# Orders at the end of the first attention and on the way to the second mixer's keys, places of two key jobs, and counts without zero matmuls

## The chip, the cores and the metric

The kernel runs on one core of a Trainium2 chip. The metric is the device time of one execution in microseconds (us). The core has engines that run side by side, each through its own list of instructions in order: TensorE (PE in the views, with its weight loads as PEld), VectorE (DVE), ScalarE (ACT), GpSimd (POOL) and SyncE (SP, which only issues DMAs here). They wait for one another on semaphores alone. TensorE writes to PSUM, from where VectorE and ScalarE take the results to SBUF.

## The reference

1024 tokens with 512 features each go through two layers of a graph network. 16384 edges (`src`, `dst`) are given, sorted by `dst`. Cut to what matters here:

```python
edge_index = jnp.stack([src, dst])
xn = _layernorm(x)
x = x + gnn0(xn, edge_index) + mixer0(xn)     # gnn0: dense attention under an adjacency mask
x = x + ffn0(_layernorm(x))                   # weight replaced by its sign, output rounded to sevenths
xn = _layernorm(x)
x = x + gnn1(xn, edge_index) + mixer1(xn)     # gnn1: 2 layers of 8-head edge attention; mixer1: linear attention
x = x + ffn1(_layernorm(x))                   # small per-row networks on nibbles

# gnn0
adj = jnp.zeros((N, N)).at[edge_index[0], edge_index[1]].set(1.0)
a = q @ k.T / sqrt(D)
a = a * adj + (1.0 - adj) * NEG
out = softmax(a) @ v
# mixer1, the second mixer
q, k, v = split(x @ Wqkv)                     # to 8 heads
q = elu(q) + 1.0;  k = elu(k) + 1.0
kv = einsum('bhnd,bhne->bhde', k, v)
z = 1.0 / (einsum('bhnd,bhd->bhn', q, k.sum(axis=2)) + 1e-06)
out = (einsum('bhnd,bhde->bhne', q, kv) * z) @ Wout + bout
# gnn1, for each of 2 layers: scores of each edge, softmax over the edges of one target, weighted sum of the values
scores = jnp.einsum('ehd,ehd->eh', q[tgt], k[srcidx])
```

How often each pair (source, target) occurs is a 1024 x 1024 table, which the kernel builds once and uses as the mask of the first attention and, in its logarithm, as the weight of each pair in the second network's attention.

## The kernel before

One function, `build`, holds a list of instructions for each engine, in the order in which its author wrote them. Nothing reorders them. What TensorE computes is cut into jobs (`JOBS`), and each has one of 4 slots of PSUM, 128 partitions x 1024 f32. A job takes the slot that comes next in turn. `begin` (on TensorE) waits until the job that had the slot before (`SLOT_BEFORE`) has been evacuated, `need` waits for the evacuated results of other jobs, and `end` signals that the slot is full:

```python
def begin(name, i):
    if SLOT_BEFORE[(name, i)]:
        wait(*evacuated(*SLOT_BEFORE[(name, i)]))
    return slot_of(name, i)
```

So a job waits for its inputs and for the evacuation of the job four places ahead of it. All matmuls are issued at L1809 and all transposes (8 of 128x128 for a slot) at L1876; a plain f32 product is split into a rounded ("high") part and a rest, so a product is three matmuls: high x high, high x rest, rest x high. The stages, in order of time:

- Start, the first mixer's preparation.
- The counts (`counts`, 8 jobs, one for each 128 targets). VectorE compares edge numbers with a ramp and gives blocks of one-hot rows in a ring (L1357, L1359, written to `PT`); TensorE multiplies two of them, 128x512 bf16 twice for a block (`count`). Each of the 8 jobs opens with two matmuls against `zeros` that start the sums, and ends with two of 8 columns that stop them. The ring is freed by `onehot_used`, which counts blocks and not the zero matmuls. Jobs of the first mixer and the attention's values stand between the 8 (`BETWEEN`).
- The first attention, by tiles n of 128 rows, with `score0(n)`, `turn0(n-2)` (transposes of the probabilities) and `attn0(n-3)` on TensorE. GpSimd makes the mask of tile n (L701, L704, L709, L710, L709 being the counts from a mask with 0 raised, of which ScalarE takes the logarithm at L952, in `KR`). VectorE multiplies the scores by the adjacency (L1394), then adds the mask and takes the row minimum (L1399, a custom instruction that has two SBUF inputs); ScalarE takes the exponential (L935, `SM`) and the high part of the turned probabilities (L943, `P0R`); VectorE takes their rest (L1406, `P0L`), and scales the rows of `attn0` (L1416) and takes their statistics. `attn0(i)` needs `P0L` of tile i. After tile 5 VectorE normalises four row tiles (L1191, to `PT`), and TensorE turns them (`xT1`).
- `AFTER_ATTN0`, the list that the change touches. `xT1(j)` and `ffn(j)` for 4 pairs j of row tiles; VectorE adds the bias (`ffn_biased`, L1452, which evacuates the job `ffn`), rounds (`ffn_quantised`, L1457 to L1459), GpSimd adds the residual (L715), VectorE takes statistics (`ffn_stats`, L1171 and after), ScalarE normalises (`normalise_pair`, L967 and L970, to `XN`), TensorE turns (`xT2(j)`), ScalarE takes the high part (`round_xT`, L824, `XTR`), VectorE the rest (`rest_of_xT`, L1205, `XTL`). Then `k1(j)` (weights `WKR` high, `WL` rest) and `v1(j)` (`QHIGH`, `QLOW`), 24 matmuls each. VectorE and ScalarE evacuate `k1` with elu (`elu_exp` L975, L1464, L1466), ScalarE evacuates `v1` (`copy_v1`, L813).
- The mixer's product and output, 361.9 to 457.3 us.
- Two layers of edge attention. `attention_order` sets the order: 64 units n a layer (a head's score tile each), with `score(n)` (matmuls of `KS` and `QS`, 6 a half), their maxima on VectorE (L1599, `nm`), the exponential on ScalarE (L1030), and after a lag of 4 units `turn` on TensorE for even n and a flip by VectorE and DMA for odd n (STREAM_TRANSPOSE, L1610, then `PT<-blocks` on SP's queue); then `agg`, a product with the values. `q` and `k` are the queries and keys of a pair of heads, 12 matmuls of `XTR`, `XTL` with `QHIGH` and `WL`; `k(0)` and `k(1)` stand ahead of the first scores, `k(2)` follows the scores of n = 4 and `k(3)` those of n = 8.

## Time and profile before

| | |
|---|---|
| median of 3 runs | 1022.92 us (1021.54 to 1023.52) |
| profiled execution, device time | 1021.41 us |
| its span in the trace | 1019.6 us |
| mean granted clock of TensorE, of 1 | 0.986 |
| TensorE busy | 951.3 us, 93% of the span, 5371 matmuls |
| VectorE busy | 625.5 us, 61% |
| ScalarE busy | 494.2 us, 48% |
| GpSimd busy | 251.1 us, 25% |
| the chain of work that ended last | PE 75%, POOL 7%, DVE 6%, issue 6%, ACT 3%, DMA 1% |

TensorE is busy nearly all the time. So a microsecond counts if it is one in which TensorE stands idle, runs at a lower clock, or does work that isn't needed. The stages end at 62.8 us (start), 182.9 (counts), 288.6 (first attention), 361.9 (keys and values of the second mixer), 457.3 (its output); the first layer of edge attention begins there and the second at 730. Times in the trace count from the span's start; the device time is 1.8 us longer than the span.

### The profile page before, as it was taken

To read this page: it belongs to the slowest core of one execution; us is meant where nothing else is said; L and a number is where in the kernel's file an instruction comes from. 1 tells how busy PE (TensorE), PEld (TensorE's weight loads), DVE (VectorE), ACT (ScalarE), POOL (GpSimd) and SP (SyncE) were. 2 spreads that over 40 slices of the span, in tenths; PEclk is the share of its full clock that TensorE was granted. 3 is DMA by queue.
4 is the path that set the end of the run, shared out by engine and by line. 5 is a ranking of instruction groups with operands and counts; after the bars stand their busy time and mean duration, and the time that the engine had idled before them with its cause. 6 is when DMAs were issued, how large, how long until landed. Compare 5 with 4: busy or idle time off the path is not lost.

```text
span 1019.6 us, 15256 instructions
## 1 busy us (share of the span) xinstructions
PE 951.3 (93%) x5371; PEld 678.4 (67%) x5378; DVE 625.5 (61%) x1087; ACT 494.2 (48%) x767; POOL 251.1 (25%) x138
## 2 busy tenths in 40 slices
PE   5999999999998999999999999999999999999915
PEld 2745545788776886886777776746777777777313
DVE  4676466558777325428667776436576666746395
ACT  1655344554724223307666666223476666651054
POOL 2000000499943051310000029112100000570400
PEclk9999999999999999999999999999999999999968
DMA  9201100000200031145655574111065665632102
GB/s 328 76 0 42 42 1 22 1 1 1 83 1 1 3 121 42 58 149 160 190 168 165 176 244 140 42 42 42 14 195 180 187 184 171 226 85 68 38 1 82
DMA packets 58848, 96.14 MB, mean 94 GB/s; under 512 B 8284, under 2 KB 38172, under 8 KB 58270
## 3 DMA queue, kind: packets, MB, share of 16 engines
q1 hardware_dynamic: 55454, 93.11, 28.4%
q10 hardware_dynamic: 3328, 2.15, 0.7%
q8 instruction: 42, 0.69, 0.3%
q14 instruction: 24, 0.20, 0.1%
HBM read 59.58 MB, written 33.55 MB: 91 GB/s over the span
## 4 chain that ended last, share of the span: by engine, by line
PE 75%; POOL 7%; DVE 6%; issue 6%; ACT 3%; DMA 1%; SPq 0%; DVEq 0%; ACTq 0%; POOLq 0%
PE slots L1809 66%; PE slots L1876 9%; POOL MASK L710 3%; POOL MASK L704 1%; POOL KR L709 1%; DMA W<-in_wkT 1%; POOL X L741 1%; POOL PT L701 1%; ACT X L1126 1%; DVE X L1694 0%; POOL WL L721 0%; DVE SM L1671 0%; DVE st L1171 0%; ACT XTR L824 0%; DVE st L1657 0%
## 5 line engine op out<-in xcount | busy, mean ns | idle before, releaser
L1809 PE MATMUL slots<-PT,XN 128*64 128x256 f32 x1024 | 117.6, 382 | 0.2 <-DMA PT<-blocks 0.2
L1809 PE MATMUL slots<-KS,QS 64*128 64x512 f32 x768 | 107.3, 406 | 4.0 <-DVE nm L1599 2.9
L1599 DVE CUSTOM_DVE_ANT_0 SM<-slots,MASK 128x1024 f32<-128x1024 f32 x64 | 75.7, 1220 | 50.6 <-PE slots L1809 50.3
L1809 PEld LDWEIGHTS slots<-PT,XN 128*64 128x64 f32 x1024 | 72.0, 137 | 42.5 <-issue 11.4
L766 POOL TENSOR_TENSOR QS<-QF,QS 128x512 fp32r<-128x512 f32 x16 | 20.7, 1292 | 319.0 <-ACT QS L1046 319.0
L1809 PEld LDWEIGHTS slots<-KS,QS 64*128 64x128 f32 x768 | 72.5, 184 | 22.9 <-issue 9.4
L1030 ACT ACTIVATE SM<-SM,nm 128x1024 f32<-128x1024 f32 x64 | 73.4, 1146 | 24.2 <-DVE nm L1599 23.6
L813 ACT ACTIVATE PT<-slots 128x1024 f32<-128x1024 f32 x68 | 69.3, 1019 | 32.0 <-PE slots L1876 27.1
L1030 ACT ACTIVATE PT<-PT,nm 128x1024 f32<-128x1024 f32 x64 | 73.3, 1145 | 14.7 <-DVE nm L1599 14.0
L1809 PE MATMUL slots<-PT 128*128 128x512 bf16 (+3 forms) x401 | 77.6, 363 | 2.7 <-ACT PT L813 1.2
L1599 DVE CUSTOM_DVE_ANT_0 PT<-slots,MASK 128x1024 f32<-128x1024 f32 x64 | 75.2, 1211 | 4.1 <-PE slots L1809 3.9
L1809 PEld LDWEIGHTS slots<-PT 128*128 128x128 bf16 (+2 forms) x408 | 36.2, 113 | 47.1 <-DVE PT L1359 20.3
L1359 DVE TENSOR_SCALAR PT<-PT 128x1024 bf16<-128x1024 f16 x148 | 63.8, 479 | 0.2 <-PE slots L1809 0.2
L701 POOL TENSOR_SCALAR PT<-PT 128x1024 f32<-128x1024 bf16 x8 | 8.4, 1048 | 184.6 <-ACT PT L929 184.1
L1876 PEld LDWEIGHTS slots<-ident,SM 128*128 128x128 f32 x376 | 41.0, 140 | 17.3 <-issue 11.5
L1876 PE MATMUL slots<-ident,SM 128*128 128x128 f32 x376 | 49.9, 277 | 2.7 <-ACT SM L1030 2.6
L1876 PE MATMUL slots<-ident,PT 128*128 128x128 f32 x356 | 45.9, 274 | 0.2 <-DVE PT L1191 0.2
L1876 PEld LDWEIGHTS slots<-ident,PT 128*128 128x128 f32 x356 | 40.4, 140 | 7.7 <-issue 2.2
L1540 DVE SCALAR_TENSOR_TENSOR XT<-slots,cols,XT 128x1024 f32<-128x1024 f32 x16 | 20.5, 1282 | 36.6 <-PE slots L1809 36.5
L1357 DVE TENSOR_SCALAR PT<-PT 128x128 bf16<-128x128 f16 x61 | 15.2, 250 | 42.5 <-PE slots L1809 42.1
L1809 PE MATMUL slots<-SXR,WL 128*128 128x512 f32 x104 | 40.8, 392 | 0.0
L1809 PE MATMUL slots<-WL,XTR 128*128 128x512 f32 x96 | 38.4, 400 | 0.0
(403 smaller groups left out, 2153.0 us busy)
## 6 DMA issues: line engine op xcount, KB each, us to landing
blocks<-FL SPq DMA_DIRECT2D x56, 512.0 KB, 3.2
PT<-blocks SPq DMA_DIRECT2D x224, 128.0 KB, 3.4
X<-in_x SPq DMA_DIRECT2D x4, 512.0 KB, 11.7
W<-in_wout SPq DMA_DIRECT2D x2, 1024.0 KB, 6.3
W<-in_gq SPq DMA_DIRECT2D x2, 1024.0 KB, 5.0
W<-in_gk SPq DMA_DIRECT2D x2, 1024.0 KB, 5.3
spill<-X SPq DMA_DIRECT2D x4, 512.0 KB, 2.6
SXR<-XTR SPq DMA_DIRECT2D x1, 2048.0 KB, 8.4
```

The costliest lines, as they stand in the source:

```text
L701: nc.gpsimd.tensor_scalar(negm[:, i % 2, :], adj0[:, i, :], -NEG, NEG, ALU.mult, ALU.add).then_inc(negm_made, 1)
L704: nc.gpsimd.tensor_tensor(MASK[:, i - 2, :], MASK[:, i - 2, :], KR[:, i % 2, :], ALU.add).then_inc(mask_made, 1)
L710: link(nc.gpsimd.tensor_scalar(MASK[:, i, :], MASK[:, i, :], 0.5, NO_EDGE, ALU.is_lt, ALU.mult))
L766: nc.gpsimd.tensor_tensor(QS[:, j % 2, 1, :], QF[:], QS[:, j % 2, 0, :].bitcast(fp32), ALU.subtract).then_inc(q_split, 1)
L813: nc.scalar.activation(dst, src, ACT.Copy).then_inc(act_evacuated, 1)
L1030: nc.scalar.activation(SMs[n % SMB], SMs[n % SMB], ACT.Exp, bias=nm[:, n % 8:n % 8 + 1], scale=-1.0, accum_out=ls[:, pair % 2, 2 * t + e:2 ...
L1357: nc.vector.tensor_scalar(dstrow[:, b, :], iota[:, t * P:(t + 1) * P], dst_f[:, bass.ds(g + b, 1)], None, ALU.is_equal)
L1359: nc.vector.tensor_scalar(srcrow[:, b, :], iota, src_f[:, bass.ds(g + b, 1)], None, ALU.is_equal).then_inc(onehot_ready, 1)
L1540: nc.vector.scalar_tensor_tensor(XT[:, c, :], src, col(bias, c), XT[:, c, :], ALU.add, ALU.add).then_inc(dve_evacuated, 1)
L1599: nc.vector.tensor_tensor_reduce(out=SMs[n % SMB], in0=src, in1=MASK[:, unit(n)[2], :], scale=-1.0, scalar=-0.1 * NO_EDGE, op0=ALU.add, op ...
L1809: return nc.tensor.matmul(o_, lhsT, rhs, start=start, stop=stop)
L1876: return nc.tensor.transpose(slot_part, src, ident[0:rows, 0:rows])
```

## The change

It has four parts; no computed value changes but for the order of the sums in `v1(0)`. GpSimd's and SyncE's instructions and their order are the same as before, and so is the number of instructions on the other engines, but for 16 fewer matmuls.

**Counts.** The two zero matmuls that open each of the 8 jobs are gone; the first block's two matmuls start the sums.

**End of the first attention.** On VectorE the rest of the turned probabilities of tile 5 goes ahead of the masked minimum of tile 7. On ScalarE the logarithm for tile 7 goes behind the exponential of tile 7 and the high part of tile 6.

**To the mixer's keys.** In `AFTER_ATTN0` the values `v1(0)` go ahead of `k1(0)`, and `k1`, `v1`, `xT2` alternate in another order. `v1(0)` issues its 16 matmuls on `XTR` first and only then waits for `XTL`, for the last 8 (`rests_last`); its start waits on ScalarE's semaphore. On VectorE `ffn_biased(0)` goes ahead of `rest_of_xT(1, 2)` and `ffn_biased(1)` ahead of `rest_of_xT(1, 3)`. On ScalarE `copy_v1(0)` and `copy_v1(1)` go ahead.

**Key jobs.** In both layers `k(2)` comes two units sooner (at n = 2, which puts it behind the first four scores and ahead of the first turn) and `k(3)` two units sooner (n = 6).

The diff, cut (the rest is shown by the words above):

```diff
@@ attention_order @@
-        if n == 4:
+        if n == 2:
             order.append(("k", 2))
-        if n == 8:
+        if n == 6:
             order.append(("k", 3))
@@ AFTER_ATTN0 @@
-               ("xT2", 0), ("k1", 0), ("xT2", 1), ("v1", 0), ("k1", 1), ("xT2", 2), ("v1", 1), ("k1", 2),
-               ("xT2", 3), ("v1", 2), ("k1", 3), ("v1", 3)]
+               ("xT2", 0), ("v1", 0), ("xT2", 1), ("k1", 0), ("v1", 1), ("xT2", 2), ("k1", 1), ("xT2", 3),
+               ("k1", 2), ("v1", 2), ("k1", 3), ("v1", 3)]
@@ ScalarE, first attention, step n @@
                 if n == TT - 1:
                     take_std(1, 0, TT // 2)
+                if n < TT - 1 or n == TT:
+                    i = min(n, TT - 1)
+                    act.wait_ge(counts_floored, i + 1)
+                    nc.scalar.activation(KR[:, i % 2, :], KR[:, i % 2, :], ACT.Ln).then_inc(logs_taken, 1)
                 if n == TT:
...
-                if n < TT:
-                    act.wait_ge(counts_floored, n + 1)
-                    nc.scalar.activation(KR[:, n % 2, :], KR[:, n % 2, :], ACT.Ln).then_inc(logs_taken, 1)
@@ ScalarE, to the keys @@
             round_xT(2, 1)
+            copy_v1(0)
             normalise_pair(2)
             normalise_pair(3)
-            for j in range(4):
+            elu_exp(0)
+            copy_v1(1)
+            round_xT(2, 2)
+            elu_exp(1)
+            round_xT(2, 3)
+            for j in range(2, 4):
                 elu_exp(j)
                 copy_v1(j)
-                if j < 2:
-                    round_xT(2, j + 2)
@@ VectorE, first attention, step n @@
                     dve.wait_ge(*evacuated("score0", n))
+                    if n == TT - 1:
+                        rest_of_probs0(n - LAG0)
                     dve.wait_ge(negm_made, n + 1)
@@ VectorE, to the keys @@
-            rest_of_xT(1, 2)
...
             ffn_biased(0)
+            rest_of_xT(1, 2)
             ffn_quantised(0)
+            ffn_biased(1)
             rest_of_xT(1, 3)
-            ffn_biased(1)
@@ TensorE, v1(0) @@
+            def rests_last(slot, wr, wl, j):
+                tiles = [(slot[:, hf * D:(hf + 1) * D], slice((2 * j + hf) * P, (2 * j + hf + 1) * P)) for hf in range(2)]
+                for dst, ts in tiles:
+                    for k in range(FC):
+                        mm(dst, XTR[:, k, ts], wr[:, k, :], k == 0, False)
+                        mm(dst, XTR[:, k, ts], wl[:, k, :], False, False)
+                need("xT2", j)
+                for dst, ts in tiles:
+                    for k in range(FC):
+                        last = mm(dst, XTL[:, k, ts], wr[:, k, :], False, k == FC - 1)
+                return last
@@ TensorE, counts @@
-                for hf in range(2):
-                    mm(slot[:, hf * D:(hf + 1) * D], zeros[:, 0:P], zeros, True, False)
...
                 for b in range(GC):
-                    count(first, b)
+                    count(first, b, b == 0)
```

Two engines at the end of the first attention. ScalarE, from the exponential of tile 6 on; `P0R` with its numbers is the high part of turned probabilities, `KR` the logarithm. Before:

```order
L935 ACTIVATE SM,ls<-SM,nm 128x1024
L943 ACTIVATE P0R_59<-slots 128x1024
L818 ACT_TABLE_LOAD
L818 ACTIVATE rstd<-rstd 128x4
L952 ACT_TABLE_LOAD
L952 ACTIVATE KR<-KR 128x1024
L935 ACT_TABLE_LOAD
L935 ACTIVATE SM,ls<-SM,nm 128x1024
L943 ACTIVATE P0R_58<-slots 128x1024
L949 ACTIVATE WL_70<-W,tiny 128x2048
```

The same piece of ScalarE's list after the change:

```order
L935 ACTIVATE SM,ls<-SM,nm 128x1024
L943 ACTIVATE P0R_59<-slots 128x1024
L818 ACT_TABLE_LOAD
L818 ACTIVATE rstd<-rstd 128x4
L935 ACT_TABLE_LOAD
L935 ACTIVATE SM,ls<-SM,nm 128x1024
L943 ACTIVATE P0R_58<-slots 128x1024
L949 ACT_TABLE_LOAD
L949 ACTIVATE KR<-KR 128x1024
L953 ACTIVATE WL_70<-W,tiny 128x2048
```

The logarithm (L952, now L949) has moved behind the exponential of tile 7 and the high part of tile 6, with no more table loads than before. VectorE on the way to the keys, `XTL` being the rests of the turned rows and the rows L1452 to L1459 those of `ffn_biased` and `ffn_quantised`, before:

```order
L1191 TENSOR_SCALAR PT<-X,mv,rstd 128x512 x4
L1205 TENSOR_TENSOR XTL<-slots,XTR 128x4x256
L1452 SCALAR_TENSOR_TENSOR SM<-slots,tiny,BC 128x1024
L1457 TENSOR_SCALAR SM<-SM 128x1024
L1458 TENSOR_SCALAR SM<-SM 128x1024
L1459 TENSOR_SCALAR SM<-SM 128x1024
L1205 TENSOR_TENSOR XTL<-slots,XTR 128x4x256
L1452 SCALAR_TENSOR_TENSOR SM<-slots,tiny,BC 128x1024
```

And after:

```order
L1196 TENSOR_SCALAR PT<-X,mv,rstd 128x512 x4
L1462 SCALAR_TENSOR_TENSOR SM<-slots,tiny,BC 128x1024
L1210 TENSOR_TENSOR XTL<-slots,XTR 128x4x256
L1467 TENSOR_SCALAR SM<-SM 128x1024
L1468 TENSOR_SCALAR SM<-SM 128x1024
L1469 TENSOR_SCALAR SM<-SM 128x1024
L1462 SCALAR_TENSOR_TENSOR SM<-slots,tiny,BC 128x1024
L1210 TENSOR_TENSOR XTL<-slots,XTR 128x4x256
```

Each of the two bias steps has moved ahead of one rest (L1205, now L1210). TensorE after the job `ffn(3)`, before (the group of three goes on to 24 matmuls):

```order
L1809 MATMUL slots<-WL_70,XTL 128x512
L1876 MATMUL slots<-ident,XN 128x128 x8
L1809 MATMUL slots<-WKR,XTR 128x512
L1809 MATMUL slots<-WL_71,XTR 128x512
L1809 MATMUL slots<-WKR,XTL 128x512
```

After the change TensorE has the values' matmuls between, of which these are the last rows:

```order
L1820 MATMUL slots<-QLOW,XTR 128x512
L1820 MATMUL slots<-QHIGH,XTL 128x512 x8
L1904 MATMUL slots<-ident,XN 128x128 x8
L1820 MATMUL slots<-WKR,XTR 128x512
L1820 MATMUL slots<-WL_71,XTR 128x512
L1820 MATMUL slots<-WKR,XTL 128x512
```

The keys' first product has moved behind `v1(0)` and the next transposes, and the products of `v1(0)` with `XTL` stand at its end.

## Rows read from the trace of the kernel before

**Rows 1.** Busy time by stretch: length, PE, PEld, DVE, ACT, POOL, clock, DMA share, GB/s.
```profile
62.80:182.90 120.10, 117.61 (x533) 63.04 (x539) 79.56 (x213) 62.29 (x163) 0.00 (x0) 1.00 0.07 23
182.90:288.60 105.70, 103.22 (x522) 86.84 (x523) 68.74 (x76) 58.94 (x58) 93.07 (x34) 1.00 0.06 21
288.60:361.90 73.30, 67.00 (x314) 54.70 (x312) 44.18 (x68) 25.26 (x31) 10.91 (x10) 0.98 0.07 25
```
**Rows 2.** One tile, PE's first counts matmuls: duration ns, first and last start, form.
```profile
L1809 PE MATMUL slots<-PT x7: 379/379/379, 62.8 to 64.1; 128*128 128x512 bf16 x7
```
**Rows 3.** Timeline, VectorE at the first counts: start, us, operation, [idle before <-releaser].
```profile
64.12 0.26 DVE L1357 TENSOR_SCALAR PT<-PT 128x128 bf16<-128x128 f16 x1 [4.25 <-PE slots L1809]
```
**Rows 4.** Timeline, TensorE's waits before the products of attention tiles 5 and 7.
```profile
268.33 0.47 PE L1809 MATMUL slots<-V0R,P0R 128*128 128x512 f32 x1 [0.91 <-DVE P0L L1406]
...
283.09 0.47 PE L1809 MATMUL slots<-V0R,P0R 128*128 128x512 f32 x1 [0.75 <-DVE P0L L1406]
```
**Rows 5.** Timeline, ScalarE at the end of the first attention.
```profile
269.71 1.06 ACT L952 ACTIVATE KR<-KR 128x1024 f32<-128x1024 f32 x1 [3.70 <-POOL KR L709]
...
272.08 1.15 ACT L935 ACTIVATE SM<-SM,nm 128x1024 f32<-128x1024 f32 x1
```
**Rows 6.** Timeline, VectorE in the first attention and just behind it.
```profile
263.63 3.41 DVE L1399 CUSTOM_DVE_ANT_0 SM<-SM,PT 128x1024 f32<-128x1024 f32 x1 [1.15 <-POOL PT L701]
...
266.97 1.22 DVE L1406 TENSOR_TENSOR P0L<-slots,P0R 128x1024 fp32r<-128x1024 f32 x1
...
275.71 4.17 DVE L1191 TENSOR_SCALAR PT<-X,mv,rstd 128x512 f32<-128x512 f32 x4
...
292.50 1.91 DVE L1191 TENSOR_SCALAR PT<-X,mv,rstd 128x512 f32<-128x512 f32 x4
...
196.94 1.23 DVE L1399 CUSTOM_DVE_ANT_0 SM<-SM,PT 128x1024 f32<-128x1024 f32 x1
```
**Rows 7.** Timeline, GpSimd beside those.
```profile
195.32 3.65 POOL L710 TENSOR_SCALAR MASK<-MASK 128x1024 f32<-128x1024 f32 x1
...
263.56 2.40 POOL L704 TENSOR_TENSOR MASK<-MASK,KR 128x1024 f32<-128x1024 f32 x1
...
269.76 3.64 POOL L710 TENSOR_SCALAR MASK<-MASK 128x1024 f32<-128x1024 f32 x1
```
**Rows 8.** Timeline, TensorE's waits on the way to the keys.
```profile
307.16 1.06 PE L1876 MATMUL slots<-ident,XN 128*128 128x128 f32 x8 [0.69 <-ACT XN L970]
310.76 0.60 PE L1809 MATMUL slots<-WKR,XTR 128*128 128x512 f32 x1 [2.53 <-DVE XTL L1205]
...
331.46 1.09 PE L1876 MATMUL slots<-ident,XN 128*128 128x128 f32 x8 [1.62 <-DVE PT L1466]
```
**Rows 9.** The chain of waits in the same stretch: start, us, what.
```profile
296.96 1.29 DVE SM L1452
...
309.39 1.24 DVE XTL L1205
...
310.76 7.31 PE slots L1809 x24
...
332.55 10.92 PE slots L1809 x48
```
**Rows 10.** Timeline, VectorE's last bias step there, of `ffn(3)`.
```profile
315.03 1.28 DVE L1452 SCALAR_TENSOR_TENSOR SM<-slots,tiny,BC 128x1024 f32<-128x1024 f32 x1
```
**Rows 11.** Busy time in one stretch, columns as in rows 1 (clock third from the end).
```profile
311.00:312.00 1.00, 1.00 (x3) 0.72 (x3) 0.96 (x3) 0.00 (x0) 0.00 (x0) 0.50 0.00 0
```
**Rows 12.** Timeline, TensorE at the start of the first layer of edge attention.
```profile
461.65 1.06 PE L1876 MATMUL slots<-ident,SM 128*128 128x128 f32 x8 [1.30 <-ACT SM L1030]
...
478.12 2.16 PE L1809 MATMUL slots<-PT,XN 128*64 128x256 f32 x18
```
**Rows 13.** Timeline, VectorE there: one score's maxima.
```profile
461.29 1.22 DVE L1599 CUSTOM_DVE_ANT_0 PT<-slots,MASK 128x1024 f32<-128x1024 f32 x1
```
**Rows 14.** DMA issues from 474.0 to 474.5 us: KB each, us from issue to landing.
```profile
PT<-blocks SPq DMA_DIRECT2D x2, 128.0 KB, 3.5
```

More of the change, by code:

```diff
@@ L1373, in _, with rest_of_probs0 @@
                 nc.vector.tensor_scalar(adj0[:, i, :], src, 1.0, None, ALU.min).then_inc(dve_evacuated, 1)
+            def rest_of_probs0(i):
+                if 0 <= i < TT:
+                    src = full(dve, "turn0", i)
+                    dve.wait_ge(p0_rounded, i + 1)
+                    nc.vector.tensor_tensor(P0L[own_p0(i)][:].rearrange("p s n -> p (s n)"), src,
+                                            P0R[own_p0(i)][:].rearrange("p s n -> p (s n)").bitcast(fp32), ALU.subtract).then_inc(dve_evacuated, 1)
             for n in range(TT + LAG0 + 1):
@@ L1401, in _ @@
                                                    accum_out=nm[:, n:n + 1]).then_inc(masked0, 1)
-                i = n - LAG0
-                if 0 <= i < TT:
-                    src = full(dve, "turn0", i)
-                    dve.wait_ge(p0_rounded, i + 1)
-                    nc.vector.tensor_tensor(P0L[own_p0(i)][:].rearrange("p s n -> p (s n)"), src,
-                                            P0R[own_p0(i)][:].rearrange("p s n -> p (s n)").bitcast(fp32), ALU.subtract).then_inc(dve_evacuated, 1)
+                if n != TT - 1:
+                    rest_of_probs0(n - LAG0)
                 i = n - LAG0 - 1
@@ L1857, in split_token_major @@
                     slot = begin(name, j)
+                    if name == "v1" and j == 0:
+                        wait(xT_rounded, 4 + j + 1)
+                        end(rests_last(slot, wr, wl, j))
+                        continue
                     need(xt, j)
@@ L2013, in _, with count @@
                 first, end_, before = ranges[t]
-                for hf in range(2):
-                    mm(slot[:, hf * D:(hf + 1) * D], zeros[:, 0:P], zeros, True, False)
-                def count(g, b):
+                def count(g, b, opens=False):
                     pe.wait_ge(onehot_ready, g + before + (b + 1))
@@ L2020, in count @@
                         last = mm(slot[:, hf * D:(hf + 1) * D], dstrow[:, b, :], srcrow[:, b, hf * D:(hf + 1) * D],
-                                  False, False)
+                                  opens, False)
                     last.then_inc(onehot_used, 1)
                 for b in range(GC):
-                    count(first, b)
+                    count(first, b, b == 0)
                 with pe.Fori(first + GC, end_, GC) as g:
```

## The prediction

> **What bounds the kernel now.** I read the busy time by stretch first. In the counts, TensorE is busy 117.61 of 120.10 us, in the first attention 103.22 of 105.70, and on the way to the keys 67.00 of 73.30, where the granted clock is 0.98 [rows 1]. No other engine comes near it but GpSimd in the first attention, with 93.07. So TensorE sets the time everywhere, and a microsecond is won only by less work on it, by a wait taken out of it, or by a higher clock. I then read its timeline for the waits that remain, and who ended them: three before products of the first attention's last tiles, all for VectorE's `P0L` [rows 4], of which the first and the last stand there; three on the way to the keys [rows 8]; one at the start of each layer of edge attention [rows 12]. The timelines of the engine named, and of the one it waited for, then tell which step of their order makes it late [rows 5 to 7, 9, 10].
>
> Two conversions are needed. A matmul is recorded as 0.38 to 0.39 us long, but the next starts earlier: 48 take 10.92 us [rows 9], 0.2275 each, so a job of 24 takes 5.46. And since records overlap by 0.16, an idle time of x in the view costs x + 0.16. Eight transposes are recorded as 1.06 [rows 8]; less the overlap with what follows they cost about 0.8.
>
> **Counts.** Removed are 2 zero matmuls in 8 jobs, 16 in all, of the same form as the counts' own. Seven of that form start between 62.8 and 64.1 us, 1.3 us for 6 steps, 0.217 each [rows 2]; 16 x 0.217 = 3.5. Are they on the path? If VectorE's one-hot rows paced this stretch, TensorE would stand idle in it, but it is idle only 2.5 us of 120 [rows 1]. VectorE waits instead: it stood idle 4.25 us at the start, until TensorE released the ring's first block at 64.12 [rows 3], which is behind two zero matmuls and two real ones. Without the zeros that release comes 0.43 sooner, so VectorE moves with TensorE. I take 3.4. Low end: if VectorE or ScalarE (79.56 and 62.29 us busy) end a few steps last between the jobs, 2.0. No loss is possible here, since nothing waits for the zeros.
>
> **End of the first attention.** The product of tile 5 starts at 268.33 after a wait of 0.91, that of tile 7 at 283.09 after one of 0.75, and one like them lies between. Two steps, each of one product and eight transposes, take 283.09 - 268.33 = 14.76; unbroken they would take 2 x (5.46 + 0.8) = 12.5. With the first wait (0.91 + 0.16) that is 3.3 us lost.
>
> Where it comes from: `P0L` of tile 5 ran at 266.97, behind the masked minimum of tile 7, which started at 263.63 and took 3.41 [rows 6] where the same instruction elsewhere took 1.23. GpSimd's L704 was running then, from 263.56 to 265.96 [rows 7]. The exponential of tile 7 ran at 272.08, behind the logarithm at 269.71, which had waited 3.70 for GpSimd [rows 5]. And the normalisation took 4.17 against 1.91 in a stretch without GpSimd [rows 6], which held back `P0L` of tile 7.
>
> After the change I lay the same durations out again. `P0L` of tile 5 takes the place at 263.3 and 1.22 us of it, done by 264.5. The minimum of tile 7 then starts inside L704, of which 1.5 us is left, and ends at about 267.1, where it did before. So TensorE finds `P0L` of tile 5 as soon as the transposes are done, at 267.2. The exponential starts at 267.2, not 272.08; the high part of tile 6 is done by 269.4, its rest by 270.7, long before TensorE comes to product 6 at 273.5. The logarithm now runs after that, to 271.7; GpSimd needs it only for its last L704, after 273.4 (the end of L710), so nobody waits. The normalisation falls to 270.8 to 272.8, beside GpSimd's L710 (269.76 to 273.40 [rows 7]) and not beside L704. `P0L` of tile 7 is then there by about 276, 3 us ahead of the product at 279.7. All three waits go: 3.3. The low end is the first rival.
>
> A minimum ran at 196.94 in 1.23 us [rows 6] while an L710 ran from 195.32 to 198.97 [rows 7], so L710 (one SBUF input) doesn't hold VectorE up as L704 (two) does. The Trainium skill, "SBUF — State Buffer", section "Who interferes with whom", calls the port pair that VectorE and GpSimd share an exclusive lock, without telling kinds of GpSimd instructions apart; by that rule this part would give next to nothing, and the row speaks against it for L710.
>
> **To the keys.** Five terms.
> (a) The first transposes of `xT2` start at 307.16 after 0.69 idle [rows 8], cost 0.85. They wait for a chain that starts with `ffn_biased(0)` at 296.96 [rows 9], which stood behind a rest (L1205, 1.24 us). Ahead of it, the chain is 1.24 sooner, more than 0.85: the wait goes, and what bounds next is TensorE itself.
> (b) `k1(0)` starts at 310.76 [rows 8]; VectorE's rest started at 309.39 [rows 9], as soon as ScalarE's high part was there. `v1(0)` now starts where that rest starts: 1.37 won. Its 8 matmuls on the rest come 16 x 0.2275 = 3.6 us later, and the rest takes 1.24, so they don't wait.
> (c) The 24 matmuls of `k1(0)` took 7.31 - 0.16 = 7.15 where 5.46 is usual [rows 9], since the granted clock was 0.50 (the level of 1.2 GHz) behind the two idle times of 0.69 and 2.53 [rows 11, 8]. I take 1.6 for it. The idle time now is about 1.2 in one piece. After the single wait of 1.62 at 331.46 [rows 8] the next 48 matmuls ran at 0.2275 [rows 9], full clock. So I take the clock to stay up.
> (d) The transposes at 331.46 waited 1.62 for the elu of `k1(0)` to free their slot, cost 1.78. In the new order their slot is that of `v1(0)`, which ScalarE copies at once, 10 us ahead. The slot of `k1(0)` goes to `xT2(3)`, 11.7 us after its end, while the elu, laid out with the trace's durations, is done some 9.3 after it: that is the cover, 2.4 us.
> (e) Added: `k1(0)` now takes the slot of `ffn(3)`, which VectorE frees at 315.03 + 1.28 = 316.31 [rows 10], less the 0.85 of (a) 315.46. TensorE would be there at 310.76 - 1.37 - 0.85 + 5.46 + 0.8 = 314.8. It waits 0.65, cost 0.8. The weights `WKR` were ready long before.
> Sum: 0.85 + 1.37 + 1.6 + 1.78 - 0.8 = 4.8. The ends: 3.2 if the clock still falls, 5.6 if (e) is hidden.
>
> **Key jobs.** At the first turn of the layer TensorE waits 1.30 [rows 12], likewise in the second layer. `k(2)`, 12 matmuls or 2.7 us, now lies in that time, and needs only the slot of the first score, free by then. But the job that stood between later scores is gone from there: scores 6 and 7 need the slots of scores 4 and 5, each freed by a maximum of 1.22 [rows 13], and by laying out VectorE's list they wait about 0.7, with 0.1 to 0.3 at two more places. By TensorE alone `agg` would start up to 0.77 sooner than 478.12 [rows 12]. It also needs blocks brought by DMA; the last are issued at about 474.2 and take 3.5 [rows 14], 477.7, and their flips move only some 0.2. So 0.2 to 0.77 a layer; I take 0.35, nearer to the DMA's end: 0.7 for two. The ends are 0 and 1.5.
>
> **Sum.** 3.4 + 3.3 + 4.8 + 0.7 = 12.2. The profiled execution of before took 1021.41, so 1009.2 by its own time. It lies 1.5 below the median of the runs shown, 1022.92, which themselves span 2.0. From the median: 1010.7.
>
> **Rivals.**
> 1. *VectorE is held up beside L710 too.* Then the normalisation ends only when GpSimd is through with L710 and the two L704 behind it, as late as before, and `P0L` of tile 7 with it; the first two waits go but the third grows by what they gave. The part gives 0.3, the time is 1013.7. For it: the normalisation was doubled once. Against it: the row at 196.94. Chance 0.12.
> 2. *The clock falls all the same* at `v1(0)`: 1.6 less, 1012.3. For it: the idle time of some 1.2 lies behind transposes and is followed by a second one of 0.65. Against: 1.62 in one piece did nothing. The Trainium skill, "TensorE: Matmul & The Clock Gate", "Part 4: PE-mode transpose", says that transposes don't count as activity for the clock; by that the idle time would be 2.0 us and not 1.2, but the same holds of the wait at 331.46. Chance 0.1.
> 3. *The counts are not bound by TensorE throughout*, and give 1 instead of 3.4: 1013. Chance 0.08.
> 4. *More than computed*: (e) hidden, the key jobs at their upper end, and the drift of later waits: 1008. Chance 0.1.
> 5. *Slower.* One mechanism: the chip grants 1.2 GHz over the new stretch and keeps it there. At that level a matmul costs 0.43, or 0.2 more. `k1` and `v1` have 192 matmuls, 38 us more: 1049. It decides from 12.2 / 0.2 = 61 matmuls at the low level on. Before, about 8 ran so, behind more idle time than is left. Chance 0.02.
> 6. *It doesn't do what it says*: waits come back at other places in both orders (the cover of 2.4 us in (d) is the thinnest), and only the counts' gain is left whole, 3 to 6 us in all: 1018. Chance 0.03, of which 0.02 within the bound of no change.
>
> **How the numbers follow.** The forecast has 0.55; the rest is above. The forecast's own spread, from its terms' ends and the 2 us between runs, is 1008.5 to 1013. The range is 1007.5 to 1015: it takes in the forecast, rivals 1 to 4, and leaves out 5 and 6 and the tails, under 2 in 10. What a measurement of this kernel can tell from no change is 0.2%, or 2 us. All cases but 5 and a part of 6 lie beyond that on the fast side: faster 0.96, same 0.02, slower 0.02.
>
> **What would show it.** In the counts, the stretch 3.4 shorter (117 us) with TensorE as busy. No wait before the products of tiles 5, 6 and 7; the normalisation at 1.9 us, not 4.2 (rival 1). Granted clock 1.00 all through the keys (rival 2), a first wait of TensorE for ScalarE's `XTR` of about 1.2, then one of 0.65 for VectorE's bias step, and none before the third transposes. The mixer's product starts at 361.9 - 3.4 - 3.3 - 4.8 = 350.4. In each layer no wait of 1.3 before the first turn, but some 0.7 before scores 6 and 7. The forecast would be wrong if VectorE's list in the counts proved to run at its own pace, or if a slot I take to be free is not.

## The result, and the profile after

| | before | changed |
|---|---|---|
| median, first series of runs | 1023.20 us (n 4) | 1013.81 us (1012.18 to 1015.92, n 4) |
| median, second series | 1023.97 us (n 11) | 1013.72 us (1013.19 to 1014.70, n 4) |
| profiled execution, device time and span | 1021.41, 1019.6 | 1012.98, 1011.2 |
| mean granted clock in it | 0.986 | 0.985 |

The ratio is 0.9909 (95% interval 0.9892 to 0.9926), and 0.9902 (0.9883 to 0.9921) the second time: 9.3 to 10.0 us faster. Forecast were 12.2 less and 1010.7, with a range of 1007.5 to 1015. So the sign came true and the time lies within the range, but the gain is 2 to 3 us short of the sum; which parts of the mechanism held is told below.

The stretches of the changed kernel, in the columns of [rows 1]. Their bounds are the same events as there (the last two are the mixer's output, and the head of the first layer of edge attention up to the first `agg`):

```profile
61.80:181.40 119.60, 117.18 (x527) 61.74 (x525) 80.43 (x213) 62.12 (x163) 0.00 (x0) 0.99 0.07 23
181.40:283.90 102.50, 102.50 (x523) 86.70 (x524) 65.67 (x76) 59.10 (x58) 91.66 (x34) 1.00 0.06 21
283.90:352.20 68.30, 65.22 (x314) 53.73 (x312) 44.12 (x68) 24.96 (x31) 12.48 (x10) 1.00 0.08 28
352.20:447.70 95.50, 94.16 (x470) 76.72 (x470) 35.27 (x35) 23.50 (x21) 33.00 (x17) 1.00 0.22 77
447.70:468.10 20.40, 19.25 (x131) 14.70 (x130) 17.77 (x27) 15.90 (x25) 1.29 (x1) 1.00 0.46 138
```

Against [rows 1] the first attention is 3.2 us shorter and the way to the keys 5.0. The counts are shorter by only half a microsecond, and their clock is 0.99 where it was 1.00. To compare stretches exactly I measure them below from TensorE's own starts: counts from the transposes ahead of them to the first of `adjT`, first attention from there to the transposes behind its last product, keys from there to the first matmul of `kv1`. Before, these are 121.23, 105.72 and 73.25.

At the end of the first attention, VectorE in the changed kernel:

```profile
261.77 1.23 DVE L1385 TENSOR_TENSOR P0L<-slots,P0R 128x1024 fp32r<-128x1024 f32 x1 [0.85 <-ACT P0R L943]
262.91 2.58 DVE L1414 CUSTOM_DVE_ANT_0 SM<-SM,PT 128x1024 f32<-128x1024 f32 x1
...
269.17 1.92 DVE L1196 TENSOR_SCALAR PT<-X,mv,rstd 128x512 f32<-128x512 f32 x4
```

ScalarE:

```profile
265.54 1.15 ACT L935 ACTIVATE SM<-SM,nm 128x1024 f32<-128x1024 f32 x1 [1.08 <-DVE nm L1414]
...
269.00 1.06 ACT L949 ACTIVATE KR<-KR 128x1024 f32<-128x1024 f32 x1
```

and GpSimd:

```profile
262.01 2.39 POOL L704 TENSOR_TENSOR MASK<-MASK,KR 128x1024 f32<-128x1024 f32 x1
...
268.21 3.76 POOL L710 TENSOR_SCALAR MASK<-MASK 128x1024 f32<-128x1024 f32 x1
```

All these rows answer [rows 5 to 7]: the exponential now waits for the minimum alone, the logarithm runs behind it, and the normalisation takes 1.92 us although an L710 runs beside it from start to end. Rival 1 is out. TensorE has no wait left before the three products, so [rows 4] has no counterpart.

On the way to the keys, TensorE's waits, to be read beside [rows 8]:

```profile
303.81 0.47 PE L1820 MATMUL slots<-QHIGH,XTR 128*128 128x512 f32 x1 [1.21 <-ACT XTR L824]
...
310.83 0.47 PE L1820 MATMUL slots<-WKR,XTR 128*128 128x512 f32 x1 [0.42 <-DVE SM L1462]
```

and at the start of the first layer of edge attention, beside [rows 12]:

```profile
457.86 0.70 PE L1820 MATMUL slots<-KS,QS 64*128 64x512 f32 x3 [0.70 <-DVE nm L1610]
...
466.39 0.51 PE L1820 MATMUL slots<-KS,QS 64*128 64x512 f32 x2 [0.44 <-DVE nm L1610]
```

The waits are those of the forecast: 1.21 for ScalarE's high part, 0.42 (said: 0.65) for the bias step, 0.70 before scores 6 and 7, and 0.44 at a later score (said: 0.1 to 0.3). The clock in the keys is 1.00. It is lower at two other places, though, where it was 1.00 before:

```profile
149.00:151.00 2.00, 2.00 (x5) 0.59 (x5) 0.38 (x2) 0.00 (x0) 0.00 (x0) 0.50 0.00 0
...
688.00:690.00 2.00, 2.00 (x6) 1.59 (x5) 1.63 (x6) 1.72 (x4) 0.00 (x0) 0.50 0.71 274
```

These are stretches of 2 us; 0.50 is the level of 1.2 GHz. Stretch by stretch of 1 us, such a drop lasts some 3.4 us and costs 1.7 us of full clock (sum of 1 - clock), like that of [rows 11]. So the time that is missing can be in the counts, in the clock, or both.

### The profile page after: what moved, and what is told of

The parts are those of the page before. It is cut to its first block, busy times and chain, and to the rows that moved or that the text cites. A ratio compares the mean times of both kernels' runs of the same rounds, so it can differ in the third digit from the quotient of the medians.

```text
span 1011.2 us, 15231 instructions
## 1 busy us (share of the span) xinstructions
PE 950.0 (94%) x5362; PEld 677.3 (67%) x5362; DVE 623.2 (62%) x1087; ACT 494.1 (49%) x767; POOL 251.4 (25%) x138
## 4 chain that ended last, share of the span: by engine, by line
PE 85%; DVE 6%; issue 3%; DMA 2%; ACT 2%; POOL 1%; SPq 0%; DVEq 0%; ACTq 0%
PE slots L1820 75%; PE slots L1904 9%; POOL X L741 1%; DMA W<-in_wkT 1%; DMA PT<-blocks 1%; ACT X L1131 1%; DVE XT L1551 0%; DVE X L1705 0%; POOL WL L721 0%; DVE SM L1682 0%; DVE XT L1572 0%; DVE st L1668 0%; DVE PT L1771 0%; DVE SM L1610 0%; SPq L607 0%
```

## Experiments

The kernels were run in series, each on one chip with runs of the kernel before between them; a table or a section compares within one series unless it names two. A single run says little here: those of before spread from 1020.6 to 1027.7 us, and follow their mean granted clock (1021.4 at 0.985, 1027.7 at 0.978). Over the 46 runs of before in three series, 0.001 of mean clock goes with 0.7 us of time (correlation -0.86); 1.0 us would be the full price, but the mean also counts the last 50 us, where a low clock costs little. The stretches of the counts, the first attention and the keys agree from kernel to kernel within 0.1 us in the trace as long as no drop of the clock falls into them, and carry the verdicts. The heads of the layers of edge attention scatter more (below).

### Each part alone

The edits are the four parts of the change, each applied alone to the kernel before.

Counts alone:

> The kernel before with the counts part alone (no zero matmuls). Theory 1, VectorE's one-hot rows set the pace in much of the counts, since at 0.4375 us a block they are slower than TensorE's 0.434, and swallow part of the 3.5 us: the stretch from the transposes ahead of the first counts to the first of adjT gets 1.5 to 2.2 us shorter in the trace, and the time 1022.9 to about 1021. Theory 2, the shortfall in the changed kernel is due to the drop of the granted clock at 148 us there: without such a drop the stretch gives the full 3.4, 1019.5. In both a run moves by 1.7 us for each drop of the clock more or less.

End of the first attention alone:

> The kernel before with the part at the end of the first attention alone. If the parts add: no wait before the products of tiles 5, 6 and 7, the stretch from the first adjT transposes to the end of the last product 3.2 us shorter, time about 1019.7. If the gain hangs on another part (a wait at the keys that grows because TensorE comes sooner), 1021 to 1023.

To the keys alone:

> The kernel before with the part on the way to the keys alone. If the parts add: the stretch from the end of the last attention product to the first of kv1 is 73.25 - 4.96 = 68.3 us, time about 1018. Of the 4.96, 1.6 to 1.7 is the granted clock; if the chip lowers it here all the same, 70, and 1019.6.

Key jobs alone:

> The kernel before with the sooner key jobs alone. Theory 1: per layer 0.27 to 0.41 us as in the changed kernel's trace, 0.7 together, which is within what can be measured: 1022.2. Rival: the first agg is bound by its DMAs and the whole is 0: 1022.9. In the trace: no wait of 1.3 before the first turn, one of 0.7 before scores 6 and 7.

| part alone | median (n) | ratio, interval | mean clock of its runs | its stretch, before and with it |
|---|---|---|---|---|
| counts | 1023.29 (12) | 0.9996, 0.9981 to 1.0012 | 0.9806 | 121.23, 118.88: 2.35 less |
| attention's end | 1019.96 (9) | 0.9970, 0.9953 to 0.9988 | 0.9826 | 105.72, 102.53: 3.19 less |
| to the keys | 1016.78 (7) | 0.9945, 0.9926 to 0.9965 | 0.9863 | 73.25, 68.32: 4.93 less |
| key jobs | 1021.04 (12) | 0.9984, 0.9969 to 0.9999 | 0.9848 | heads of the two layers: 20.82, 20.63 and 20.86, 20.84 |

(Before: 1023.73 median of 28 runs, mean clock 0.9826.) The second and third part have their full gain alone, in the trace to 0.05 us of what they have together. They don't depend on one another. The counts part takes 2.35 us out of its stretch without any drop of the clock there, so the drop isn't what hid the gain in the changed kernel, and theory 2, with its full 3.4, falls. Theory 1 is right that part of the 3.47 removed doesn't come through, but 1.1 us are missing and not 1.3 to 2.0, and the next sections show that VectorE's pace isn't the cause it took it for. And yet the time of this kernel hardly moves, since its runs had a mean clock lower by 0.0020, which is 1.4 to 2 us. The key jobs alone give 0.2 us in the trace, and 1021.04 by a clock that was higher by 0.0022. That 0.2 is the lowest of many: in the ten kernels that have the sooner key jobs the head of the first layer takes 20.35 to 20.63 us, mean 20.42, in the four that don't 20.81 to 20.89, and that of the second 20.28 to 20.95, mean 20.51, against 20.86 to 20.91 and once 21.61. So the part is worth 0.4 a layer.

### The changed kernel again, and without the counts part

```diff
+                for hf in range(2):
+                    mm(slot[:, hf * D:(hf + 1) * D], zeros[:, 0:P], zeros, True, False)
...
-                    count(first, b, b == 0)
+                    count(first, b)
```

> The changed kernel unaltered, beside the three others of this call and more runs of before, because single runs differ by 1.7 us or a multiple with each drop of the granted clock. If the parts add with the gains of the stretches seen so far (2.35 counts, 3.2 end of attention, 4.95 keys, 0.4 key jobs, 10.9 together) and drops are as frequent as before: 1012.8 against 1023.7. If more drops come with it, as in the kernel with the counts part alone, 1 to 2 us more.

> The changed kernel with the zero matmuls back. Theory 1, the counts part shortens its stretch by 2.35 but brings more drops of the clock (mean clock 0.9806 with it alone against 0.9826 before), which gives about 2 back: this kernel then takes within 0.7 us of the changed one, with a higher mean clock by about 0.002. Theory 2, the lower clock with the counts part was chance: it is 2.35 us slower than the changed kernel, at the same mean clock.

Measured: 1013.72 (4 runs, clock 0.9837) and 1016.56 (6 runs, 1013.01 to 1019.35, clock 0.9835; ratio 0.9925, 0.9903 to 0.9947). Without the counts part it is 2.8 us slower at the same mean clock, where theory 2 expected 2.35 and theory 1 at most 0.7. Runs of this kernel spread over 6 us, so the difference is uncertain by about 1 us (one standard error). It speaks for theory 2: the part is worth about its 2.35, and in the changed kernel it doesn't lower the clock. Why the kernel that had it alone ran at 0.9806 isn't shown.

### What holds up the counts

The lengths of the 8 counts jobs (start of the job to the start of what follows it, from TensorE's starts) were shorter in the kernel with the counts part alone by 0.27, 0.43, 0.17, 0.44, 0.44, 0.44, 0.10 and 0.15 us; two matmuls are 0.43. In job 0, 0.17 of the 0.43 is missing; VectorE waits on the ring once there, for 0.10, and I did not follow it further. Jobs 2, 6 and 7 have in common that TensorE's product just ahead, `v0(1)`, `q0(2)` or `q0(3)`, is rounded by ScalarE. TensorE's weight loads at job 6 (PEld), before:

```profile
164.71 2.27 PEld L1809 LDWEIGHTS slots<-PT 128*128 128x128 bf16 x12 [0.26 <-issue]
167.22 0.20 PEld L1809 LDWEIGHTS slots<-PT 128*128 128x128 bf16 x2 [0.23 <-DVE PT L1359]
```

The same with the counts part alone, 3 us sooner:

```profile
161.95 1.84 PEld L1809 LDWEIGHTS slots<-PT 128*128 128x128 bf16 x10 [0.26 <-issue]
164.46 0.11 PEld L1809 LDWEIGHTS slots<-PT 128*128 128x128 bf16 x2 [0.67 <-DVE PT L1359]
```

and ScalarE there:

```profile
162.15 1.11 ACT L880 ACTIVATE Q0R<-slots,rl 128x1024 fp32r<-128x1024 f32 x1 [6.55 <-PE slots L1809]
163.17 0.97 ACT L907 ACTIVATE PT<-PT 128x128 bf16<-128x128 f16 x3
164.04 0.60 ACT L912 ACTIVATE PT<-PT 128x128 bf16<-128x128 bf16 x2
```

TensorE's own row there names ScalarE as what it waited for:

```profile
164.47 3.22 PE L1809 MATMUL slots<-PT 128*128 128x512 bf16 x16 [0.18 <-ACT PT L912]
```

ScalarE makes part of the one-hot rows (L907, L912), and starts on them only when it has rounded the product, 1.11 us. That start hangs on the product, not on the zeros. TensorE uses up the first five blocks (10 weight loads), which need nothing of ScalarE, 0.43 sooner without the zeros, and its weight loads then wait 0.67 instead of 0.23: of the 0.43 the wait takes back nearly all. The test moves the rounding behind ScalarE's loop:

```diff
+            late_ones = []
             for t in range(TT):
...
+                for name, i in late_ones:
+                    if name == "q0":
+                        round_query(i)
+                    else:
+                        src = full(act, "v0", i).rearrange("p (t d) -> p t d", t=2)
+                        nc.scalar.activation(V0R[:, 2 * i:2 * i + 2, :], src, ACT.Copy).then_inc(v0_rounded, 1)
+                late_ones = []
                 copy_out(MASK[:, t, :], "counts", t)
...
+                    elif name == "v0" and i == 1:
+                        late_ones.append((name, i))
...
                     elif name == "q0":
-                        round_query(i)
+                        late_ones.append((name, i))
```

> The changed kernel, with ScalarE's rounding of v0(1), q0(2) and q0(3) moved behind its loop of the next counts job. Theory: in the counts jobs 2, 6 and 7 the zeros lay beside ScalarE, which first rounds the product before (1.0 to 1.1 us) and only then makes its share of the one-hot rows, so only 0.17, 0.10 and 0.15 of 0.43 came through. With the rounding out of the way the missing 0.26, 0.33 and 0.28 come, 0.9 together: the stretch from the transposes ahead of the counts to adjT 118.0 without a drop of the clock. Rival: VectorE's pace is the limit there, and nothing changes, 118.9. In the times 0.9 is near what can be told.

Jobs 2, 6 and 7, each up to the start of what follows it, take 6.81, 5.02 and 6.56 us, against 7.07, 5.37 and 6.83 with the counts part alone: 0.26, 0.35 and 0.27 less, expected were 0.26, 0.33 and 0.28. Job 3, which had nothing to win, stays at 7.13 to 7.14. The weight loads at job 6 now start the same way without a wait of that size:

```profile
165.01 2.27 PEld L1830 LDWEIGHTS slots<-PT 128*128 128x128 bf16 x12 [0.26 <-issue]
167.58 1.00 PEld L1830 LDWEIGHTS slots<-PT 128*128 128x128 bf16 x6 [0.30 <-issue]
```

The theory holds. Two drops of the clock fell into the stretch, at 93 and 151 us, so it is 121.26 long. Jobs 1 and 5, in which they lie, are 1.65 and 1.69 longer than with the counts part alone; without that it is 117.9, where 118.0 was expected. The time is 1011.86 (4 runs; before 1024.68 in this series, ratio 0.9873, 0.9844 to 0.9901), 1.9 less than the changed kernel had in the other series. By the trace 0.9 of it is this; the rest lies within the spread of four runs.

### Without `rests_last`

```diff
-                    if name == "v1" and j == 0:
-                        wait(xT_rounded, 4 + j + 1)
-                        end(rests_last(slot, wr, wl, j))
-                        continue
```

> The changed kernel without rests_last: v1(0) waits for VectorE's XTL as the other products do. By the sum, 1.37 us come back at the start of v1(0) (idle 2.5 in one piece instead of 1.2), of which the wait of 0.58 before k1(0) hides so much that 0.8 is left; and if the drop of the clock hangs on a wait of that length, it comes back too, 1.7 more: the stretch to kv1 69.1 or 70.8, in place of 68.29.

The stretch to `kv1` is 70.57 us: a wait of 2.54, and the clock drops behind it.

```profile
305.69 0.47 PE L1820 MATMUL slots<-QHIGH,XTR 128*128 128x512 f32 x1 [2.54 <-DVE XTL L1210]
...
306.73 0.63 PE L1820 MATMUL slots<-QHIGH,XTR 128*128 128x512 f32 x1
```

70.57 is 2.28 more than 68.29. The drop is 1.7 of it, so 0.6 is left for the wait. But the time is 1013.32 (4 runs, clock 0.9838, ratio 0.9895, 0.9876 to 0.9914), no slower than the changed kernel at 1013.72. In this profile the drop at 688 us isn't there; it is as if a drop taken away here were found again elsewhere. That is the next question.

### Where the clock drops

From the 14 profiles, one of each kernel and two of the changed one, in stretches of 1 us, with the drops of the last 50 us left out, where TensorE is mostly idle:

| place | drop in the profile of | none in that of |
|---|---|---|
| first product behind `xT2(0)`, where TensorE waited about 2.5 us (306 to 318 us) | before, counts alone (twice as long), attention's end alone, key jobs alone, without `rests_last` | none of those with that wait |
| the same place with a wait of 1.2 | none | all nine |
| the first attention's last products, behind waits of 0.48 and 1.27 (276 to 281) | logarithm back | none of those with these waits |
| the same, with waits of at most 0.92, or none | none | all thirteen others |
| second layer's values, behind a wait of 2.14 (687 to 700) | changed, changed again, without counts, counts alone, keys alone, logarithm back | before and five others |
| the same, that wait filled (next section) | none | both |
| in the counts (92 to 100, 148 to 158) | eleven of fourteen | before, counts alone, keys alone |

A drop behind the 2.5 us wait came in 5 of 5 profiles, and in 0 of 9 once the wait was 1.2. So in its place my term (c) is right. That doesn't make 1.2 us a length after which the clock stays up: in the kernel with the logarithm back it fell behind 1.27, with transposes and a wait of 0.48 just ahead. What the profiles leave out is the second line of evidence: the mean clock of all runs. Before has 0.9826 (28 runs), 0.9821 (11) and 0.9814 (7), the changed kernel 0.9822 (4) and 0.9837 (4), without `rests_last` 0.9838 (4). Pooled, that is 0.9823 before and 0.9830 changed, at most 0.7 us, where a drop of 1.7 us fewer would be 0.0017. Eight runs leave the mean uncertain by some 0.0007 (one standard error), so this alone tells neither 0 nor 1.7 us apart. All kernels with the wait of 2.5 us at that place (83 runs) have 0.9825, all with 1.2 us (31 runs; the two of the next section and the single run with the logarithm back left out), 0.9839: 0.0013 apart with a standard error of 0.0005, or 0.9 to 1.4 us. That speaks for a net gain, but single kernels lie further apart than their runs explain (0.9806 counts alone, 0.9848 key jobs alone, both with 2.5 us), so its size stays open.

Part of it may come back later in the run. Of the five kernels that had the drop at the keys one had one at the second layer's values; of the seven others with the wait of 2.14 five had. That is too few to tell from chance (such a split or a clearer one comes in about 1 of 8 cases).

### The wait at 685 us filled

```diff
+                idle = begin(f"gv{l}", 0)
+                for _i in range(7):
+                    mm(idle[:, 0:D], wr[:, 0, 0:P], wr[:, 0, :], True, True)
                 for i, c in enumerate(ROUND_ORDER):
                     wait(state_rounded, i + 1)
```

> The changed kernel with 7 matmuls whose sums are thrown away, put into TensorE's wait of 2.14 us ahead of the second layer's values (at 685 us). Theory 1, the granted clock drops there in half of the profiles because TensorE stands idle: no drop there, the mean clock 0.001 higher, 0.8 us won on average. Theory 2, drops come about equally often whatever is removed, and move to another place: mean clock and time as in the changed kernel, 1013.8.

> Both of the two before together, the candidate for a version faster than both. Sum of the two by theory 1: 1013.8 - 0.9 - 0.8 = 1012.1; by the rivals 1013.8.

In the changed kernel TensorE stands idle at that place:

```profile
687.07 0.47 PE L1820 MATMUL slots<-GV1R,SXR 128*128 128x512 f32 x1 [2.14 <-issue]
```

The sums of the seven matmuls are overwritten. In the profile of both together, TensorE at that place, and the stretch behind it:

```profile
685.27 2.19 PE L1830 MATMUL slots<-GV1R 128*128 128x512 f32 x7
687.93 0.50 PE L1830 MATMUL slots<-GV1R,SXR 128*128 128x512 f32 x1 [0.47 <-ACT SXR L1107]
```

```profile
687.00:690.00 3.00, 2.53 (x11) 1.75 (x11) 2.93 (x4) 3.00 (x3) 0.00 (x0) 1.00 0.88 298
```

No drop there in either profile; with 6 of 12 before, two without one come by chance in 1 of 4 cases. The times: 1012.76 filled (1010.12 to 1015.14, clock 0.9837, ratio 0.9875, 0.9843 to 0.9906); 1010.95 with the late rounding too (1009.79 to 1012.89, clock 0.9850, ratio 0.9865, 0.9833 to 0.9897). Filling the wait alone can't be told from nothing: the kernel with the late rounding alone had the same mean clock. But the one with both is the fastest of all, 2.8 us below the changed kernel by the medians of different series, and by the ratios 0.9865 against 0.9902 and 0.9909, whose intervals overlap at the edges; against the late rounding alone (0.9873) no gain is shown. In both profiles drops lay in the counts, at 93 and 151 us, in that of the filled wait alone the second twice as long, so those places, not this one, are what is left.

### One step further at the keys

```diff
-            ffn_quantised(2)
             ffn_biased(3)
+            ffn_quantised(2)
```

> The changed kernel with VectorE's ffn_biased(3) ahead of ffn_quantised(2), which frees the slot that the first product of k1(0) waits for 2.1 us sooner. If that slot is all it waits for: the wait of 0.42 goes, the stretch to kv1 is 68.29 - 0.58 = 67.7, the time 0.6 less. Rival: the pair 2 gets normalised 1.3 us later, the third transposes wait for it, and nothing is won, 68.3 or more.

The wait of 0.42 goes, and the keys' first product starts 0.66 sooner after `v1(0)`. Then `v1(1)` waits for VectorE, which comes later to the rest of the second pair:

```profile
PE slots L1820 <- ACT XTR L824: 1.2, 1, 1.2
...
PE slots L1820 <- DVE XTL L1210: 0.2, 1, 0.2
```

(TensorE's waits in that stretch: total, times, longest.) `k1(0)` and what follows up to the third transposes take 11.48 us instead of 10.97, of which 0.35 is this wait, seen from start to start. Net, the stretch is 68.12, only 0.17 less. Neither of my two cases: the slot was what it waited for, and a wait took its place, but for another tile than the rival had. The time, 1013.39 (6 runs), can't tell such a size.

### The logarithm back in its place

The changed kernel with ScalarE's part of the end of the first attention undone, VectorE's kept:

> The changed kernel with ScalarE's logarithm of tile 7 back ahead of the exponential of tile 7. By my layout VectorE's half alone takes only the first wait away (1.07): the exponential of tile 7 again starts near 272, the products of tiles 6 and 7 wait for their rests, and the stretch of the first attention is about 104.6 us, between the 102.5 of the changed kernel and the 105.7 of before. Rival: VectorE's order alone carried the gain, and it stays 102.5 to 103.

It ran once, at 1019.16 us, so the trace alone can tell. The stretch is 106.34 with a drop of the clock at 276 us in it. The clock drops behind two waits that came back, the second of 1.27:

```profile
273.96 1.09 PE L1903 MATMUL slots<-ident,SM 128*128 128x128 f32 x8 [0.48 <-ACT SM L935]
276.32 0.47 PE L1819 MATMUL slots<-V0R,P0R 128*128 128x512 f32 x1 [1.27 <-DVE P0L L1384]
```

and the normalisation is slow again, since it now falls beside L704:

```profile
276.29 4.14 DVE L1195 TENSOR_SCALAR PT<-X,mv,rstd 128x512 f32<-128x512 f32 x4
```

Less 1.7 for the drop that would be 104.6, what was laid out. But the drop can't be taken off whole. It slowed the product of tile 6, and meanwhile the rest of tile 7 got ready, for which the product of tile 7 would otherwise have waited, as it does before:

```profile
282.27 1.23 DVE L1384 TENSOR_TENSOR P0L<-slots,P0R 128x1024 fp32r<-128x1024 f32 x1
...
284.29 0.48 PE L1819 MATMUL slots<-V0R,P0R 128*128 128x512 f32 x1
```

The same rest before:

```profile
281.72 1.22 DVE L1406 TENSOR_TENSOR P0L<-slots,P0R 128x1024 fp32r<-128x1024 f32 x1
```

With the logarithm back the rest ends at 283.50. Before, it ended at 282.94, and the product started at 283.09, 0.15 later [rows 4]. With the same 0.15 the product would start at 283.65 here without the drop, 0.64 sooner than it did, and the stretch would be 105.7 (an estimate), which is that of before. So VectorE's order without ScalarE's is worth about nothing, not the 1.1 that I laid out: the exponential of tile 7, at 272.66, is as late as before (272.08 in a trace that runs 0.6 ahead there), and everything behind it with it. With VectorE's order in place ScalarE's carries the whole 3.2. ScalarE's order without VectorE's was not run.

The port rule of the Trainium skill, "SBUF — State Buffer", section "Who interferes with whom", fits the 4.14 beside L704 and not the 1.92 beside L710. The section does tell GpSimd instructions that read SBUF from those that only write it, which the prediction passes over; L704 and L710 both read it, so that doesn't explain the difference.

## Why the prediction was right where it was, and where it wasn't

| step | forecast | measured in the trace |
|---|---|---|
| counts | 3.4 (2.0 to 3.5) | 2.35 alone; 0.76 in the changed kernel's profile, with a drop of the clock in it |
| attention's end | 3.3 | 3.19 alone, 3.20 changed |
| to the keys, with (c) | 4.8 (3.2 to 5.6) | 4.93 alone, 4.96 changed |
| key jobs, two layers | 0.7 (0 to 1.5) | 0.2 alone; 0.41 + 0.27 changed, 0.47 + 0.55 again; 0.8 by all profiles |
| sum | 12.2 | 11.2 to 11.5 at equal clock elsewhere |
| the clock elsewhere | as before | two drops in each profile of the changed kernel, none in that of before |
| time | 12.2 less | 9.4 less, 10.3 less again |

**The attention's end and the keys** came out as laid out for the whole part, and so did the waits that were to be left or new. The split between the two engines, which the prediction doesn't give, I had wrong in the last experiment. The method was the same both times: take each instruction's duration from a row where nothing interferes, follow the new order, and ask what the engine beside it is running. The normalisation at 1.9, the cover of L710, the thin cover of (d): all held.

**The counts** are the term that was mis-sized, 2.35 for 3.4, still above its low end. The step that failed is "if VectorE's rows paced this stretch, TensorE would stand idle in it". A matmul is recorded 0.38 us long and the next can start 0.217 after it, so a record hides a wait of up to 0.16. The weight loads show what TensorE's own row doesn't. Before, in the counts:

```profile
PEld slots L1809 <- DVE PT L1359: 20.3, 73, 0.7
```

Of these 73 idle times TensorE's row shows hardly one. Their sum is no loss, though: most lie under a product that is still running. With the counts part alone the sum is larger, 22.5 us, and the stretch 2.35 shorter. They only show the places; what TensorE lost there is read from the lengths of the jobs. And the text set the release of the ring as all that the one-hot rows wait for. It left out ScalarE, which makes a share of them behind the rounding of the product ahead. The low end allowed for it without naming the place. Rival 3 (2.4 less by this part) took the right direction and over twice the size.

**The clock** is the rest, and the error of method: the sum took one drop out and assumed the others to stay as they were. In the profile of before there is one drop outside the end, that of [rows 11]; in the two of the changed kernel it is gone, and there are two others, one in the counts and one at the second layer's values. In the two spans that closes the account: 11.2, less two drops at 1.6 each as the stretches show them, is 8.0; with 0.8 won at the start by a DMA that came sooner (the counts begin at 60.9 to 61.7 us in the 14 profiles, latest in that of before) and 0.4 lost, 0.3 of it behind the second layer's head, it is 8.4, the difference of the spans. The medians, 9.4 and 10.3 less, lie between 8.0 and 11.2.

The means of all runs give an account that rests on no single profile. Before has 1023.9 (46 runs), the changed kernel 1013.9 (8), 10.0 less with a standard error of 0.5. The stretches without the clock give 2.35 + 3.2 + 3.3 + 0.8 = 9.65. So some 0.4 is left for the clock where the sum had 1.6, and with the 1.05 missing in the counts that is the shortfall of 2.2. Whether the drops left over come more often because of the change, or would have come anyway in other runs of before, isn't settled: the mean clock over all runs is 0.0007 higher, not lower. What is shown is that the gain of removing one can't be read from one profile. The profiled execution of before was also a good one, 1021.41 where the median of 28 was 1023.73, with clock 0.986 against a mean of 0.9826.

Rival 2, the clock falling all the same at `v1(0)`, didn't come: after 1.2 us of waiting there no drop came in nine profiles. "Part 4: PE-mode transpose" of the Trainium skill's "TensorE: Matmul & The Clock Gate" says that transposes don't count as busy in the same way. These runs don't settle whether that matters. Counted so, the idle time at 273.5 to 276.3 with the logarithm back is 2.8 us, and a drop followed; that from 329.8 to 332.3 before is 2.5 (1.62 and eight transposes), and none followed.

## What to carry to other kernels

To see whether another engine paces TensorE, don't rest on its busy share, because matmul records overlap and hide short gaps. The waits of its weight loads show the places, and the length of each job, before and after, what they cost. When work is taken off the engine that sets the time, ask for each place what starts its feeders: a feeder that starts on an earlier event (here ScalarE's rounding) doesn't move with it, and takes the gain back as a wait. A drop of the clock in a stretch can also hide a wait, so its price can't simply be taken off the stretch: redo the order of the starts. And a term that rests on the granted clock should be priced by the mean clock of many runs, not by the one drop that a profile happens to show.

## What the runs showed of the hardware that I had not expected

The drops of the clock come at a few places, each in some executions and not in others: in the counts in eleven of fourteen profiles, at the second layer's values in six of twelve with the wait of 2.14. Only behind the wait of 2.5 us were they there every time. Each lasts 3.4 us or twice that, and costs up to 1.7 us or twice that; with the mean clock goes most of the spread of 1020 to 1028 us between runs of the kernel before. Two of the places are in the counts, where TensorE's record shows no idle time: the drops around 150 us begin in or just behind eight products with 34 rows of contraction, and TensorE counts as busy 2.00 of 2.00 us there; those around 93 us begin behind some 30 products of only 32 columns.
